# Attention chances: the normalising multiply moved between engines, and part of the side matmuls placed ahead of the value products

## What is computed

```
x = x + xattn(layernorm(x), ctx)          # 4 batches, 512 tokens + 64 context rows, D = 1024
x = x + ffn(layernorm(x))                 # int8-style fake quantisation of weights and activations

q = latents @ Wq.T ; k, v = [context, latents] @ Wk.T, Wv.T      # 16 heads of 96, 4 key/value heads
scores = q k^T / sqrt(96)                 # 512 x 576 per head
attn   = softmax(scores, axis=-1)
out    = (attn @ v) @ Wo.T
```

## Time and profile before

| | |
|---|---|
| median of 3 runs | 1688.86 us (1684.45 to 1690.93) |
| the profiled execution | 1685.0 us, span 1683.2 us |
| TensorE, busy in the span | 1552.1 us (92%), mean granted clock 0.964 |
| DVE, ACT, POOL busy | 1086.0, 670.2, 745.3 us |
| DMA engines, 60 to 1155 us | 0.93 busy |

### The profile page before, as it was taken

One profiled execution on the slowest core, in us unless ns is written; L12 is line 12 of the kernel. 1 busy time (PEld: TensorE's weight loads), 2 busy tenths in 40 slices (PEclk: granted clock), 3 DMA queues, 4 the chain that ended last, 5 costly groups with the idle time before them and its releaser, 6 DMA issues. The chain is left out here.

```text
span 1683.2 us, 24162 instructions
## 1 busy us (share of the span) xinstructions
PE 1552.1 (92%) x8084; PEld 770.0 (46%) x8084; DVE 1086.0 (65%) x2208; ACT 670.2 (40%) x1180; POOL 745.3 (44%) x827
## 2 busy tenths in 40 slices
PE   6989989999987999898899899988689999999997
PEld 3534434654433465444346444444344444444443
DVE  5355775346566535567644557673669999898984
ACT  3356655156555415655532655662211111111110
POOL 3378888058868506777840677781000000000000
PEclk9989989999998999999999999999889999999998
DMA  7299999489999949989985999996932333333332
GB/s 243 75 233 222 233 243 235 149 217 228 208 232 233 249 146 226 243 189 254 241 209 187 267 229 242 221 246 173 368 101 75 89 94 79 103 79 103 79 84 62
DMA packets 529805, 310.93 MB, mean 185 GB/s; under 512 B 473904, under 2 KB 480816, under 8 KB 528560
## 3 DMA queue, kind: packets, MB, share of 16 engines
q1 hardware_dynamic: 529712, 309.76, 75.0%
HBM read 139.20 MB, written 46.66 MB: 110 GB/s over the span
## 5 line engine op out<-in xcount | busy, mean ns | idle before, releaser
L790 POOL TENSOR_TENSOR p_f<-p_f,small 128x576 f32<-128x576 f32 x256 | 299.2, 1169 | 373.3 <-ACT p_nat L1010 372.5
L792 POOL TENSOR_TENSOR p_nat<-p_f,p_nat 128x512 f16<-128x512 f32 x256 | 312.5, 1221 | 20.1
L999 ACT ACTIVATE p_f<-ps_s,small 128x576 f32<-128x576 f32 x256 | 188.4, 736 | 209.0 <-DVE small L1112 208.3
L1112 DVE TENSOR_REDUCE small<-ps_s 128x1 f32<-128x576 f32 x256 | 192.3, 751 | 111.9 <-PE ps_s L904 110.6
L903 PE MATMUL ps_s<-k,q 96*128 96x512 f16 x768 | 226.0, 387 | 39.4 <-ACT p_f L999 39.2
L1010 ACT ACTIVATE p_nat<-p_f,small 128x576 f16<-128x576 f32 x256 | 195.5, 774 | 149.7 <-DVE small L1120 113.7
L1386 PE MATMUL ps_gu<-w_gu_sb,xT 128*128 128x512 bf16 (+1 forms) x1152 | 230.9, 361 | 0.3 <-DMA w_gu_sb<-gu_q 0.3
L1427 ACT ACTIVATE g_sb<-g_sb,sx 128x512 f32<-128x512 f32 (+1 forms) x128 | 74.6, 583 | 393.0 <-DVE g_sb L1498 335.0
L1365 POOL TENSOR_TENSOR rstd<-var_eps,minus_half 128x1 f32<-128x1 f32 x16 | 8.8, 550 | 458.9 <-DVE var_eps L1468 458.9
L918 PE MATMUL ps_o<-pT,v_lo 128*96 128x512 f16 x320 | 132.6, 414 | 39.6 <-DMA pT<-p_nat 39.5
L1399 PE MATMUL ps_d<-w_dn_sb,hT 128*128 128x512 bf16 x704 | 161.2, 382 | 5.3 <-DMA hT<-h_int 5.3
(11 more groups left out here) (114 smaller groups left out, 2448.2 us busy)
## 6 DMA issues: line engine op xcount, KB each, us to landing
w_in<-w_gu SPq DMA_DIRECT2D x40, 512.0 KB, 4.7
wq<-wq_c SPq DMA_DIRECT2D x36, 512.0 KB, 4.7
wo<-wo_c SPq DMA_DIRECT2D x24, 768.0 KB, 5.7
gu_q<-w_t SPq DMA_DIRECT2D x44, 256.0 KB, 4.2
w_in<-w_dn SPq DMA_DIRECT2D x8, 1376.0 KB, 7.0
w_gu_sb<-gu_q SPq DMA_DIRECT2D x3, 2816.0 KB, 12.7
x_acc<-x SPq DMA_DIRECT2D x4, 2048.0 KB, 8.4
x<-x_acc SPq DMA_DIRECT2D x8, 1024.0 KB, 5.1
```

Source lines behind the costliest of these rows:

```text
L790: nc.gpsimd.tensor_tensor(f, f, inv_sum[:, j % 2, t:t + 1].broadcast_to([P, S]), ALU.mult).then_inc(p_scaled, 1)
L792: nc.gpsimd.tensor_tensor(h[:, S + C:2 * S], f[:, 0:T], h[:, 0:T], ALU.subtract)
L999: nc.scalar.activation(p_f[:, t % NF, :], scores(t), ACT.Exp, bias=neg_max[:, j % 2, t:t + 1], accum_out=sums[:, j % 2, t:t + 1]).then_inc ...
L1112: nc.vector.tensor_reduce(neg_max[:, j % 2, t:t + 1], scores(t), AX.X, ALU.max, negate=True).then_inc(mx_done, 1)
```

## The change

Two things are changed.

First, `chances_lo` loses its multiply. A new POOL operation `chances_scaled` multiplies the float32 tile by the reciprocal and by 512 in one tensor-scalar instruction, in place; it waits for the reciprocal. `chances_hi` on ACT then waits for POOL's result and is a plain copy to fp16. `chances_lo` waits for the copy and keeps the two subtractions. DVE's scaling of the sum by 1/512 goes. Due times become `scaled` +2.4, `high` +3.7, `low` +4.6.

Second, in `step_order` the first third of a step's side units (rounded down) stands ahead of the value products, for steps under 16.

```
+HIGH, LOW = 3.7, 4.6
...
-    work = [("PV", j - 2, t) for t in range(ST)] if j >= 2 else []
-    work += [("X", u, i) for u in side_work(j, b) for i in range(parts(u))]
+    side = [("X", u, i) for u in side_work(j, b) for i in range(parts(u))]
+    values = [("PV", j - 2, t) for t in range(ST)] if j >= 2 else []
+    n = len(side) // 3 if j < STEPS - 2 else 0
+    work = side[:n] + values + side[n:]
...
-                act += [(t + 1.0, "exp", b, j, k), (t + 2.4, "high", b, j, k)]
-                pool.append((t + 3.1, "low", b, j, k))
+                act += [(t + 1.0, "exp", b, j, k), (t + HIGH, "high", b, j, k)]
+                pool += [(t + 2.4, "scaled", b, j, k), (t + LOW, "low", b, j, k)]
...
+            def chances_scaled(b, j, t):
+
+                f = p_f[:, tile(b, j, t) % NF, :]
+                pool.wait_ge(inv_done, tile(b, j, t) + 1)
+                nc.gpsimd.tensor_scalar(f, f, inv_sum[:, j % 2, t:t + 1], P_UP, ALU.mult, ALU.mult).then_inc(p_scaled, 1)
+
             def chances_lo(b, j, t):
-
-                f, h = p_f[:, t % NF, :], p_nat[:, t % NN, :]
+                f, h = p_f[:, tile(b, j, t) % NF, :], p_nat[:, t % NN, :]
                 pool.wait_ge(p_high, tile(b, j, t) + 1)
-                nc.gpsimd.tensor_tensor(f, f, inv_sum[:, j % 2, t:t + 1].broadcast_to([P, S]), ALU.mult).then_inc(p_scaled, 1)
-                pool.wait_ge(p_scaled, tile(b, j, t) + 1)
                 nc.gpsimd.tensor_tensor(h[:, S + C:2 * S], f[:, 0:T], h[:, 0:T], ALU.subtract)
...
-                act.wait_ge(inv_done, tile(b, j, t) + 1)
+                act.wait_ge(p_scaled, tile(b, j, t) + 1)
...
-                nc.scalar.activation(p_nat[:, t % NN, 0:S], p_f[:, t % NF, :], ACT.Copy,
-                                     scale=inv_sum[:, j % 2, t:t + 1]).then_inc(p_high, 1)
+                nc.scalar.activation(p_nat[:, t % NN, 0:S], p_f[:, tile(b, j, t) % NF, :], ACT.Copy).then_inc(
+                    p_high, 1)
...
-                s = sums[:, j % 2, t:t + 1]
-                nc.vector.tensor_scalar(s, s, 1.0 / P_UP, None, ALU.mult).then_inc(sum_down, 1)
-                dve.wait_ge(sum_down, tile(b, j, t) + 1)
-                nc.vector.reciprocal(inv_sum[:, j % 2, t:t + 1], s).then_inc(inv_done, 1)
+                nc.vector.reciprocal(inv_sum[:, j % 2, t:t + 1], sums[:, j % 2, t:t + 1]).then_inc(inv_done, 1)
```

More of the change, by code:

```diff
@@ L477, in attention_phase @@
         v_done = sem("v_done")
-        sum_down = sem("sum_down")
         inv_done = sem("inv_done")
@@ L784, in context_lo @@
                     ctx_lo, 1)
+            def chances_scaled(b, j, t):
+                f = p_f[:, tile(b, j, t) % NF, :]
+                pool.wait_ge(inv_done, tile(b, j, t) + 1)
+                nc.gpsimd.tensor_scalar(f, f, inv_sum[:, j % 2, t:t + 1], P_UP, ALU.mult, ALU.mult).then_inc(p_scaled, 1)
             def chances_lo(b, j, t):
-                f, h = p_f[:, t % NF, :], p_nat[:, t % NN, :]
+                f, h = p_f[:, tile(b, j, t) % NF, :], p_nat[:, t % NN, :]
                 pool.wait_ge(p_high, tile(b, j, t) + 1)
-                nc.gpsimd.tensor_tensor(f, f, inv_sum[:, j % 2, t:t + 1].broadcast_to([P, S]), ALU.mult).then_inc(p_scaled, 1)
-                pool.wait_ge(p_scaled, tile(b, j, t) + 1)
                 nc.gpsimd.tensor_tensor(h[:, S + C:2 * S], f[:, 0:T], h[:, 0:T], ALU.subtract)
                 nc.gpsimd.tensor_tensor(h[:, S:S + C], f[:, T:S], h[:, T:S], ALU.subtract).then_inc(p_low, 1)
-            run = {"power": power, "tokens_lo": tokens_lo, "context_lo": context_lo, "low": chances_lo}
+            run = {"power": power, "tokens_lo": tokens_lo, "context_lo": context_lo, "scaled": chances_scaled, "low": chances_lo}
             context_lo(None)
@@ L998, in chances @@
                     act.wait_ge(p_low, n - NF + 1)
-                nc.scalar.activation(p_f[:, t % NF, :], scores(t), ACT.Exp, bias=neg_max[:, j % 2, t:t + 1],
+                nc.scalar.activation(p_f[:, tile(b, j, t) % NF, :], scores(t), ACT.Exp, bias=neg_max[:, j % 2, t:t + 1],
                                      accum_out=sums[:, j % 2, t:t + 1]).then_inc(p_done, 1)
             def chances_hi(b, j, t):
-                act.wait_ge(inv_done, tile(b, j, t) + 1)
+                act.wait_ge(p_scaled, tile(b, j, t) + 1)
                 if head(b, j):
```

## The result

The changed kernel takes 1662.8 us (median of 4 runs, 1658.15 to 1667.15) beside 1689.9 us for the kernel before in the same comparison. The ratio is 0.9843, with a 95% interval of 0.9824 to 0.9861: 1.6% or some 26 us faster, where 15 were forecast. Its profiled execution took 1660.82 us, span 1659.0. The profiled execution of the kernel before (1685.0 us) lies 4 to 8 us under that kernel's medians (1688.9 to 1692.8 in the different comparisons), so a difference read between its profile and another comes out some 5 us smaller than the timed one.

The account below looks back on a forecast made before the run. It took TensorE, with waits at PV0 and score tiles, as the bound. From the profiled 1685.0 us, -13.1 and -2 gave 1669.9; 3.9 more for the runs' median gave 1673.8, so 1674 us, range 1657 to 1705.

Parts of the forecast that it names:

- the larger gain: Rival: every transpose goes out earlier and score-tile waits fall too, giving 1659 us; chance 0.12.
- What bounds: Attention phase: TensorE bounds, with 39.5 us of waits at PV0 and 39.2 at score tiles; short steps full.
- Part 1: Reorder of side work ahead of the value products: -13.1 us, bounds -2 and -17.7.
- 14.1 us of cover: PV0 waits in steps 6, 11, 12 and 15 hidden by side work put ahead: 14.1 of 17.1 us.
- give-back: Steps 11 to 15: TensorE comes early to score tiles and waits longer there, losing half of 9.1 us, 4.5.
- 3.6 us of low clock: Two PV0 waits of over 2 us vanish, each sparing about 1.8 us of low clock behind it: 3.6 us.
- Part 2: Multiply first on POOL, ahead of ACT's copy: -2 us, bounds -12 and the slower rival.
- x: Time of POOL's new one-input multiply: taken as 0.75 us, bounds 0.6 and 1.15.
- the first product of this part: Remaining TensorE waits: 30 places × 0.6 us earlier × 0.39 of transposes helped = 7 us gained.
- 5 us taken back for the coupling: ACT's high half now waits for POOL, holding ACT's queue when POOL is behind: 5 us lost.
- The slower rival: POOL becomes the bound in short steps when x exceeds 0.85: near 1700 to 1715 us; chance 0.22.
- The transfers take it back: Rival: DMA engines and SP stay late, so the saving is lost: 1687 us; no-change chance 0.24.

Follow-up runs that it names:

- the kernel without pairs: Changed kernel with subtractions due at 3.2, not 4.6, so on POOL no tile's multiply stands ahead of another's subtractions; 0.9975 of the kernel before.
- the one with more load: Changed kernel plus a POOL fill of 256 elements behind each tile's subtractions and their signal; 0.9923 of the kernel before.
- this part alone: Changed kernel with the old step order, so only the multiply by reciprocal and 512 first on POOL; 0.9907 of the kernel before, about 16 us faster.
- the one-input multiply alone: Kernel before with POOL's two-input multiply made a one-input tensor-scalar, still behind ACT's high half, old order; 0.9931 of the kernel before, about 12 us faster.
- at x = 1.15: Changed kernel with POOL's multiply made two-input again and DVE's scaling of the sum put back; 1.0069 of the kernel before.
- Together with the new order: Kernel before with the new step order and the one-input multiply on POOL at its old place behind ACT's high half; 0.9874 of the kernel before.
- the order alone: Kernel before with the new step order only, the multiply staying on POOL behind ACT's high half; 0.9934 of the kernel before, about 11 us faster.
- every tile pipelined: Changed kernel with subtractions due at 6.4, not 4.6, so in 218 tiles the next multiply stands ahead of them; 1.0079 of the kernel before.

## Why the prediction was right, and where its sizes were off

The direction and the range (1657 to 1705) hold, and so does the outline: two parts that add, with POOL's queue close to the pace of the short steps. The size does not: 1662.8 is below the 1665 to 1680 that the prediction kept for its forecast and among the times that it gave to the larger gain, at 0.12. That rival is not what happened either, since waits at score tiles did not fall (39.2 to 40.4 us). Taking it step by step:

- **What bounds.** Right: TensorE with two kinds of waits, and full short steps. The nearness of POOL's pace in the short steps showed in the kernel without pairs and in the one with more load. That the transfers make these steps full was not tested.
- **Part 1**, -13.1: right in size, measured 11 alone, but with luck, since its terms do not hold one by one. The 14.1 us of cover became 17.1; the give-back was 12 and not 4.5, and sits in other places than assumed; the 3.6 us of low clock were not seen with this part. In the profile that leaves 6 us. The lower bound of 2 does not follow from the terms either: with all of the 9.1 given back, 8.6 are left. That the clock is low behind each wait of over 2 us was too simple: behind the 3.40 us at 846.18 it stayed at 1.00 for the next 10 us, and behind the 2.49 us at 419.82 it fell only after 1.2 us.
- **Part 2**, x: taken as 0.75 from the one-input row; median 0.745, mean 0.80. The Trainium skill's page "GPSIMD Engine Reference", section 4.1, has a one-input operation at roughly line rate, and a two-input one about twice as slow as on VectorE. No run here has this multiply on VectorE, so that factor is not tested; on GpSimd itself the one-input form is the quicker, 0.745 against 1.15 us for the same 576 elements, a factor of 1.5.
- **Part 2**, -2 us: this is the term that was mis-sized; alone it measures 16. The 0.6 us for an undisturbed tile is right (4.76 to 4.08), but it was used for all tiles. The median from exponential to the end of the subtractions fell by 1.7 us for tiles 0 (6.8 to 5.1) and by 1.1 for the others (5.7 to 4.6), since before each waited for the tile ahead on POOL. The waits of TensorE fell by about what the first product of this part said (7 us; 4.8 and 2.8 in the profile with this part alone). The second fault is the clock, which was put at nothing here: busy time fell by 4.3 us with this part alone, and by 6.0 with the one-input multiply alone. The third is the 5 us taken back for the coupling: in the changed order multiplying first gains 5 (0.9874 to 0.9842). The rest of the 16 is not placed.
- **The slower rival** was real and close: at x = 1.15 the same change is 0.7% slower than before. Its threshold of 0.85 came from a step cost that was 0.6 us too high; from the measured 4.31 and 2.94 I estimate x = 0.75 + (11.2 - 10.2) / 4 = 1.0. By the same sum POOL's step at 1.15 is 10.2 + 4 × 0.4 = 11.8 us, 0.6 over TensorE's 11.2 or 17 us in 28 short steps; they grew by 27, so POOL's pace is not the whole cost. The kernel without pairs crosses the same line from the other side (11.7 against 11.2).
- **The transfers take it back** did not happen: the DMA share rose to 0.96 and time fell with it.
- **The signs.** Those for right came: PV0 waits of moved steps at 0.5 us, x at 0.745, the clock at 0.97, 4.1 us for the undisturbed tile. One for wrong came by half: ACT's high half waited for POOL 232.6 us, over the 200 named, but beside score-tile waits that stayed (39.2 to 40.4). No PV0 wait turned up in steps 7 to 9.

What stays open: by which waits of TensorE the one-input multiply alone gains. Its profile has 40.3 and 37.3 us of waits, as before, and 6.0 us less busy time for the same matmuls (1023.5 against 1029.5), with 55.7 us of it at the low clock against 68.1. The clock bears this out over the timed runs: its mean is 0.9675 in the six of this kernel and 0.9635 in the eleven beside them, which is 14 us less at the low level and at most 7 us of time. So about half of the 12 us came through the clock; why it fell less often, with waits as long as before, is not shown. Together with the new order the busy time is 1027.1, and TensorE is idle 5 us less than with the order alone.

## What to carry to other kernels

When an engine's queue is near the pace of the bound, value a shorter instruction by what it does to queueing and not by one undisturbed tile: 0.4 us less on POOL for each of 256 tiles gave 12 us. Beside the waits, count what TensorE's clock can give back: 8 of the 24.5 us in the profile here. An operation split around another engine's (multiply, copy, subtract) costs the round trip in queue time, unless the next tile's work stands in the gap and is already ready there. Work pulled ahead of a wait paid in the steps with more side work and not in the short ones, and each pulled piece must be checked for its own inputs: units of the next batch, one in each of three steps, cost 12 us.

## What the runs showed of the hardware

GpSimd's tensor-scalar with two operations on 128 x 576 float32 takes 0.745 us (median), whether the second factor is 512 or 1.0, against 1.15 us for the two-input product of the same size. ScalarE's copy of 128 x 576 float32 from SBUF to fp16 takes 0.68 us without a per-partition scale and 0.78 with one. TensorE's busy time for the same matmuls of the attention phase moved between 1018 and 1036 us from one kernel to another, mostly but not only with the time at the low of the two clock levels, 1.2 GHz: of the busy time, 68.1 us before, 51.3 in the changed kernel and 78.1 with every tile pipelined.
